# Three preparations moved in the order of a hand-scheduled two-layer kernel

## The reference

```
h = layernorm(x) * (1 + ca) + sa;  x = x + ga * attention(h)
h = layernorm(x) * (1 + cb) + sb;  x = x + gb * ffn(h)
```

## Time and profile before

| | us |
|---|---|
| median of three runs | 1192.31 |
| the profiled execution, whole | 1189.56 |
| its span | 1187.6 |
| PE busy | 1076.4 (91%) |
| DVE busy | 875.5 (74%) |
| ACT busy | 524.6 (44%) |
| POOL busy | 170.6 (14%) |

### The profile page before, as it was taken

The page is one execution under the profiler, slowest core; times in us unless marked ns, Lnnn a source line. Parts: engine busy times, 40 slices in busy tenths (PEclk is TensorE's granted clock), DMA queues, the critical chain, the costliest instruction groups (busy, mean ns, idle before and its releaser), DMA issues. The chain is left out here.

```text
span 1187.6 us, 12949 instructions
## 1 busy us (share of the span) xinstructions
PE 1076.4 (91%) x4313; PEld 522.3 (44%) x4360; DVE 875.5 (74%) x1606; ACT 524.6 (44%) x1100; POOL 170.6 (14%) x143
## 2 busy tenths in 40 slices
PE   6788778799988899879998999999998999999997
PEld 3435655444433444334443354443444444444443
DVE  4887876667766788887688799587897677785654
ACT  3655653355434475254263363154444163531421
POOL 3100000102111322121121131122102000100100
PEclk9877865599998999999999999999999999999999
DMA  8411110433300332223130103013110011020000
GB/s 273 178 54 36 54 37 24 171 89 107 107 18 1 121 100 84 85 61 115 55 94 19 27 27 98 2 50 98 34 62 10 1 54 36 18 71 0 1 36 35
DMA packets 47571, 75.53 MB, mean 64 GB/s; under 512 B 8369, under 2 KB 16049, under 8 KB 47377
## 3 DMA queue, kind: packets, MB, share of 16 engines
q1 hardware_dynamic: 47216, 74.62, 19.8%
q0 software_dynamic: 288, 0.09, 0.2%
HBM read 66.16 MB, written 8.54 MB: 63 GB/s over the span
## 5 line engine op out<-in xcount | busy, mean ns | idle before, releaser
L1501 PE MATMUL g_g<-h,wt 128*128 128x512 f16 x1728 | 404.6, 383 | 5.2 <-DVE hid L1804 2.0
L1501 PEld LDWEIGHTS g_g<-h,wt 128*128 128x128 bf16 (+1 forms) x1728 | 168.7, 99 | 225.2 <-issue 38.7
L1515 PE MATMUL g_d<-wt,parts 128*128 128x512 bf16 (+1 forms) x831 | 200.2, 382 | 7.5 <-DVE tmp L1634 2.7
L2118 ACT ACTIVATE parts<-hid 128x512 f16<-128x512 f32 x108 | 68.0, 629 | 301.6 <-DVE hid L1804 301.6
L1424 PE MATMUL g_o<-shared 128*128 128x512 f32 x384 | 181.2, 615 | 14.4 <-DVE tmp L1595 6.4
L1797 DVE SCALAR_TENSOR_TENSOR hid<-th,g_g 128x512 f32<-128x512 f32 x108 | 73.5, 680 | 132.7 <-ACT th L2111 132.5
L1515 PEld LDWEIGHTS g_d<-wt,parts 128*128 128x128 f16 x864 | 83.6, 99 | 113.9 <-issue 15.4
L2228 POOL TENSOR_TENSOR acc<-acc,sqh 128x512 f32<-128x512 f32 x52 | 77.3, 1486 | 298.8 <-ACT sqh L2124 298.8
L1424 PEld LDWEIGHTS g_o<-shared 128*128 128x128 f32 x384 | 74.4, 198 | 97.3 <-issue 71.5
L1809 DVE TENSOR_TENSOR parts<-hid,parts 128x512 f16<-128x512 f32 x108 | 88.4, 819 | 26.0 <-ACT parts L2118 25.9
L2211 POOL TENSOR_TENSOR g_rstd<-g_var,g_power 128x4 f32<-128x4 f32 x20 | 24.2, 1210 | 333.3 <-DVE g_var L1541 333.3
(11 more groups left out here) (319 smaller groups left out, 1517.5 us busy)
## 6 DMA issues: line engine op xcount, KB each, us to landing
shared<-in_w SPq DMA_DIRECT2D x48, 256.0 KB, 2.7
x<-in_codes SPq DMA_DIRECT2D x32, 264.0 KB, 3.1
w_raw<-in_wt SPq DMA_DIRECT2D x16, 512.0 KB, 3.5
x<-in_wmod SPq DMA_DIRECT2D x7, 1024.0 KB, 5.3
wmod<-in_wmod SPq DMA_DIRECT2D x5, 1024.0 KB, 11.5
codes_f<-x SPq DMA_DIRECT2D x32, 132.0 KB, 1.7
gates<-in_x SPq DMA_DIRECT2D x4, 1024.0 KB, 8.2
x<-in_x SPq DMA_DIRECT2D x4, 1024.0 KB, 6.8
```

Source lines behind the costliest of these rows:

```text
L1501: mm = nc.tensor.matmul(pg[i][:], wide[:, k, o:o + P], h16[f % 2][:, s, k], start=(s == 0 and k == 0), stop=(s == 1 and k == KD - 1))
L1515: mm = nc.tensor.matmul(pd[j][:], parts16[:, t % 3, s, j * P:(j + 1) * P], wd[:, m, :], start=(m == 0 and s == 0), stop=(done and s == 1))
L2118: nc.scalar.activation(parts16[:, t % 3, 0], hid[:, t % 2], ACT.Copy).then_inc(hi_ready, 1)
```

## The change

Three numbers in `PREP`, and the key by which the uses of `xn` are sorted. Phase 2's preparation (the third group) begins at third 51 in place of 74, phase 4's at 174 in place of 179, and phase 6's at 242 in place of 245. The sort key of the first-layer preparations is now `PREP[f] + 10`, close to where their norm stands; with 51 in the table the bare number would have put the third group's norm ahead of the norm of the first layer-1 attention (54), while in the program it comes behind it. The order of the twelve uses is the same as before.

```
-    PREP = (None, 26, 74, 122, 179, 201, 245, 278)
+    PREP = (None, 26, 51, 122, 174, 201, 242, 278)
...
-    norms = sorted([(PREP[f] or 0, ("x", f)) for f in range(2 * NG)] + [(ATT[i], ("y", i)) for i in range(NG)])
+    norms = sorted([((PREP[f] or 0) + (10 if 0 < f < NG else 0), ("x", f)) for f in range(2 * NG)] + [(ATT[i], ("y", i)) for i in range(NG)])
```

## The result

The changed kernel took 1196.76 us (median of 20 runs) against 1190.34 for the kernel before (20 runs): a ratio of 1.0049, 95% interval 1.0032 to 1.0066. It is slower by about 6 us, where 7 us faster was forecast.

What follows compares the result with a forecast made beforehand. PE, busy 91%, was the bound, so only its standstills and slow passes could be won. Phase 2 (+14 - 0.8 - 14.1 - 5.0 = -5.9), phase 4 (-0.5) and phase 6 (-0.6) gave -7.0: 1185.3 us, range 1176 to 1197.

Steps and rivals of the forecast that it cites:

- the yardstick: Tiles 46 to 48, a bare layer-1 attention cycle of three tiles and three projections: 25.8 us of PE work, 25.90 measured.
- Stretches B, C and D: Tiles 24 to 26, 27 to 29 and 30 to 32, which phase 2's work leaves: -0.8, -14.1 and -5.0 us.
- Stretch A: Tiles 17 to 23, which take in phase 2's moved work: +14 us on 53.48, bounds +4 and +18.
- the walk through the lists: Tiles 17 to 23 followed through the engines' lists: +1.2 in 17 and 18, +10 in 19 to 21, +2.8 in 22 and 23.
- Phase 4, -0.5: Tiles 58 to 64: 2.2 us off for two PE waits at the norm's place, 1.7 added for statistics and rows.
- Phase 6, -0.6: Tiles 80 to 85: rows leave a tile full on DVE, modulations leave relu and exp; -0.6 us, between -1.9 and +1.5.
- The transfer of `x`: Second launch: lands after 6.8 us, first block due some 18 us after tile 17's start, so no wait.
- the slower one: Tiles 17 to 23: attention projections alternate with transposes for two banks and wait; cost 26.8 us, +5.8 in all, 1198; chance 0.15.
- The same bill in another place: Tiles 17 to 23 pay what tiles 27 to 32 paid, 19 to 20 us; -1 in all, 1191; chance 0.28.
- "More": DVE's 8.1 us idle in tiles 17 to 23 fill up, which then cost +6; -15 in all, 1177; chance 0.12.
- The holds of DVE by POOL: Tiles 22 and 23: four POOL low halves slow two-input DVE operations, at most 3.8 us dearer; left at zero.
- The clock: Tile 20: slow PE passes behind both new waits, twice 1.97 us less one in tiles 27 to 29, net +2.

Runs made afterwards that it cites:

- both kinds of bank wait are repaired: Kernel before with phase 2 at 51, its blocks read one third sooner, its transposes three thirds later, phase 6 at 242: 1184.31 against 1191.40, ratio 0.9939.
- the run without additions: Phase 2 at 51 with blocks read one third sooner, minus the third group's additions to x and row statistics: tiles 19 and 20 took 18.05 against 19.63.
- phase 4 alone: Kernel before with only phase 4's preparation moved to third 174 (and the new sort key): 1196.38 against 1189.99, ratio 1.0041.
- the repaired reader: Phase 2 at 51, transposes three thirds later, phase 6 at 242, third and fourth groups' blocks read one third sooner, against kernel before: 1174.50 against 1191.40.

## Why the prediction was wrong, point by point

- **What bounds the kernel, and the yardstick**: right. C came down to 25.22, the bare cycle's 25.8 or so.
- **Stretches B, C and D**: right, off by 0.1, 1.3 and 0.0 us.
- **Stretch A, +14**: mis-sized; it was +23.0. Taken with B it was 22.2 against my 13.2. Once both kinds of bank wait are repaired 11.1 + 1.7 = 12.8 is left, so the waits and the slow passes behind them cost 9.4 together (4.2 in A for the blocks' banks alone, 4.5 net for the transposes' alone), where I had 1.5 + 2 = 3.5. The moved work itself was 12.8 where I had the other 9.7. Of the miss of 9.0, 5.9 are waits and 3.1 are work; that my whole sum of 13.2 is close to the 12.8 is luck. I also took the work to be DVE's: the run without additions showed PE's own projections to hold tiles 19 and 20.
- The step that failed there was the walk through the lists: for tile 20 it had two of the waits nearly right (1.5 and 2; measured 1.92 and 2.01), but it let DVE's idle time be filled by the blocks, while each wait of PE delays the next tanh and with it opens new idle on DVE; DVE's idle rose from 8.1 to 15.7 (76.48 - 60.81). And for tiles 22 and 23 it counted ACT's modulations only as time (+2.8, measured +7.9), not as readers of a bank that a projection stands in line for.
- **Phase 4, -0.5**: wrong, +6.1. I took off PE's two waits at the norm's old place as if they were the norm's, and did not look for the same pairing at the new one: a transpose unit, and a projection two units behind it (a wait of 5.33). That term, put at nothing, is the larger part of the whole loss. The statistics and rows cost +1.5, the place of the transposes 4.6.
- **Phase 6, -0.6**: right, -1.0 in the tiles named, -0.5 with tile 86.
- **The transfer of `x`**: right, no wait for it in tile 19.
- **Rivals**: the slower one, with its mechanism (alternation for two banks) and its price of 26.8 in A for the measured 23.0, came nearest: 1198 forecast, 1196.76 measured. It got 0.15. But its loss was to lie in A alone, and tiles 17 to 32 together cost only 1.9: the loss is phase 4's, which no rival named. The total is near by luck. The argument against this rival, that C had shown only two waits, was read from a place with other neighbours. The same bill in another place (A 19 to 20) is nearly as close for phase 2 by itself. "More", with A at +6, is excluded.
- **The holds of DVE by POOL**: put at zero, and open. DVE's busy time in A rose by 15.4 (60.81 - 45.37), not by the 12.2 counted. Most of the difference are operations that ran beside one of POOL's and took longer than their like: the four rows 2.87 in place of 1.92 (2.2 in my count), line 1868 1.64 in place of 0.68 as in the earlier trace rows, line 1856 0.94 in place of 0.17, line 1586 0.82 in place of 0.42. What of it reached A's length no run tested.
- **The clock**: in A five groups took 5.33, 2.79, 1.44 and twice 1.11 where their like took 3.70, 1.89, 1.12 and 0.66, 3.8 us in all; C and D saved some 3.2 of the same kind. So the net was about +0.6, where +2 was priced. That price came from the Trainium skill (TensorE: Matmul & The Clock Gate, "HAM oscillation — how this bites in real kernels"), by which a PE that waits is throttled again and starts its next work cold. The trace agrees in A (granted clock 0.66 behind the wait of 2.01), but the last section has a wait of 3.21 behind which the clock did not fall.

## What to carry to other kernels

Where side work shares a few banks in turn, moving a block does not move only its busy time: look at which unit stands two places behind it at the new place, and behind what in its own list the reader of the bank stands there. Try a reader one step sooner before trying another place; here one number on DVE's side, for two groups, gave most of 1.2% at the old place, while moving the block gave nothing that can be told from zero. And when a wait is taken off at the old place, search for it at the new one.

## What the runs showed of the hardware

A standstill of PE of the same 3.15 us was followed by slow matmuls of different extent in different executions. In one with the same list of instructions up to there (phase 4 alone), the eight passes that took 5.40 in the earlier trace rows took 6.68:

```profile
489.94 6.68 PE L1424 MATMUL g_o<-shared 128*128 128x512 f32 x8 [3.15 <-DVE tmp L1595]
```

Tile 27 was then 21.1 long in place of 19.8. Tile 30 shows the whole width. The two kernels at the old place have one list up to there. With the reader sooner for the third group (PE, then the stretch as above):

```profile
527.13 0.66 PE L1318 MATMUL g_o<-ident,xn 128*128 128x128 f32 x4 [3.21 <-ACT hf L2021]
527.62 3.69 PE L1424 MATMUL g_o<-shared 128*128 128x512 f32 x8
```

```profile
523.92:531.31 7.39, 4.18 (x13) 2.05 (x14) 5.59 (x6) 5.09 (x9) 3.58 (x3) 1.00 0.65 178
```

and for the third and fourth:

```profile
524.54 1.12 PE L1318 MATMUL g_o<-ident,xn 128*128 128x128 f32 x4 [3.22 <-ACT hf L2021]
525.45 6.10 PE L1424 MATMUL g_o<-shared 128*128 128x512 f32 x8
```

```profile
521.32:531.55 10.23, 7.01 (x14) 3.33 (x14) 4.67 (x6) 5.10 (x9) 3.75 (x3) 0.67 0.66 205
```

After the same wait the clock stayed at its upper level once and fell once, and the tile took 13.12 or 15.94. Tile 43 took 19.9, 20.7, 21.1 or 21.5 in kernels that have no edit in it. From tile 17 on, a tile behind no standstill has one length wherever its list and its neighbours' are unchanged. So a bank wait of some 3 us in this kernel costs its own time and 0 to 3 us of PE at its lower clock behind it, and brings a scatter of that size into the timing; behind shorter waits it varied too (none behind 1.92 and 1.7 behind 2.01 in tiles 19 and 20; tile 83, behind a wait of 1.89, took 10.3 or 12.0). A single profiled execution can't tell a gain of 1 or 2 us in such a tile.

The granted clock of tile 43's stretch, before and with the repaired reader:

```profile
648.62:669.73 21.11, 18.34 (x47) 7.31 (x49) 12.01 (x17) 5.41 (x10) 1.26 (x1) 0.84 0.10 26
```

```profile
647.68:661.35 13.67, 13.62 (x47) 5.36 (x47) 11.95 (x17) 6.79 (x12) 1.51 (x1) 1.00 0.15 40
```
